# Weight quantization of a transformer layer: three operations a chunk for four, and chunks in sixteen groups of six for four of 24

## The reference

```python
x = _layernorm(x + attn(x, head_dim_mask, w_q, w_k, w_v, w_o))
x = _layernorm(x + ffn(x, w_gate, w_up, w_down))

def _weight_quant(w):        # forward value: wq
    scale = 1.0 / jnp.clip(jnp.mean(jnp.abs(w)), 1e-05)
    wq = jnp.clip(jnp.round(w * scale), -1.0, 1.0) / scale
def _act_quant(x):
    scale = 127.0 / jnp.clip(jnp.max(jnp.abs(x), axis=-1, keepdims=True), 1e-05)
    xq = jnp.clip(jnp.round(x * scale), -128.0, 127.0) / scale
gate = silu(act_quant(x) @ weight_quant(w_gate).T);  up = act_quant(x) @ weight_quant(w_up).T
out  = act_quant(gate * up) @ weight_quant(w_down).T
```

## Time and profile before

| | |
|---|---|
| median of 3 runs | 4197.9 us (4190.73 to 4200.52) |
| profiled execution | 4206.66 us, span of the slowest core 4205.1 us |
| spans of the 8 cores | 4170.1 to 4205.1 us |
| phase AB / C1 and C2 in that span | 1563.4 us / 2641.7 us |
| busy shares in the span | PE 50%, PEld 22%, DVE 56%, ACT 13%, POOL 5% |
| DMA | 440.44 MB, mean 105 GB/s |
| second pass over the weights | DVE 814.8 to 919.4 us and three more stretches like it, the last to 1471.7 us |

### The profile page before, as it was taken

How to read it: one execution, slowest core, us unless ns; L and a number is a source line. 1 busy time by engine, 2 the same in 40 slices (tenths; PEclk the granted TensorE clock), 3 DMA queues, 4 the chain that set the end, 5 groups by cost and what they waited for, 6 DMA issues and landing times. The chain is left out here.

```text
span 4205.1 us, 32766 instructions; the slowest of 8 cores (4170.1 to 4205.1 us)
## 1 busy us (share of the span) xinstructions
PE 2109.6 (50%) x8516; PEld 943.0 (22%) x8516; DVE 2353.7 (56%) x3982; ACT 535.4 (13%) x794; POOL 217.5 (5%) x295
## 2 busy tenths in 40 slices
PE   3625235233241508384747565665747155555555
PEld 2311112111010103232323222222223122222222
DVE  2154661777778755757575766666666522333333
ACT  0211112111020201111111111111111100000000
POOL 1000000111110100000000000000000000000000
PEclk8655555555555559697878778787969577887777
DMA  8315330353443624343333334333423332222222
GB/s 244 116 36 175 115 115 20 95 155 113 127 143 102 182 67 126 91 117 94 100 106 99 105 90 120 83 118 80 130 70 91 96 99 75 85 80 80 80 80 85
DMA packets 290772, 440.44 MB, mean 105 GB/s; under 512 B 12960, under 2 KB 220832, under 8 KB 290592
## 3 DMA queue, kind: packets, MB, share of 16 engines
q1 hardware_dynamic: 250000, 319.32, 25.8%
q0 software_dynamic: 40592, 119.03, 9.7%
HBM read 337.64 MB, written 100.66 MB: 104 GB/s over the span
## 5 line engine op out<-in xcount | busy, mean ns | idle before, releaser
L929 PE MATMUL ps_y<-wdq,hqr 128*128 128x512 bf16 x2048 | 478.6, 397 | 381.4 <-DMA hqr<-hqTs 375.7
L779 PE MATMUL ps_g<-wgu,xqr 128*128 128x512 bf16 x2048 | 495.9, 386 | 132.3 <-issue 92.6
L785 PE MATMUL ps_u<-wgu,xqr 128*128 128x512 bf16 x2048 | 485.1, 380 | 0.0
L799 PE MATMUL ps_t<-identb,hq 128*128 128x128 bf16 x1024 | 129.5, 307 | 582.3 <-DVEq L739 456.1
L53 DVE SCALAR_TENSOR_TENSOR z2t<-ps_y,yscale,x1r 128x512 f32<-128x512 f32 x64 | 48.0, 751 | 561.2 <-PEq L934 482.9
L929 PEld LDWEIGHTS ps_y<-wdq,hqr 128*128 128x128 bf16 x2048 | 205.6, 101 | 654.2 <-issue 438.7
L53 DVE TENSOR_SCALAR gtr<-ps_g,scv 128x512 f32<-128x512 f32 x256 | 192.1, 750 | 249.1 <-PEq L790 248.7
L566 PE MATMUL ps_h<-pbuf,vtok 128*128 128x512 f32 x256 | 195.9, 765 | 244.7 <-ACTq L54 244.7
L53 DVE TENSOR_TENSOR hp<-sgt,ps_u 128x512 f32<-128x512 f32 x256 | 176.0, 687 | 242.5 <-ACTq L54 242.5
L779 PEld LDWEIGHTS ps_g<-wgu,xqr 128*128 128x128 bf16 x2048 | 184.4, 98 | 439.2 <-issue 262.7
L53 ACT ACTIVATE sgt<-gtr 128x512 f32<-128x512 f32 x256 | 161.1, 629 | 873.8 <-DVEq L54 873.8
(11 more groups left out here) (102 smaller groups left out, 2287.0 us busy)
## 6 DMA issues: line engine op xcount, KB each, us to landing
wgu<-wgqs SPq DMA_DIRECT2D x64, 1024.0 KB, 7.8
wgu<-wuqs SPq DMA_DIRECT2D x64, 1024.0 KB, 10.1
wstf<-wgT SPq DMA_DIRECT2D x64, 512.0 KB, 4.9
wstf<-wuT SPq DMA_DIRECT2D x64, 512.0 KB, 4.6
wstf<-wdT SPq DMA_DIRECT2D x64, 512.0 KB, 3.8
hqTs<-hqts POOLq DMA_DIRECT2D x32, 1024.0 KB, 8.7
hqr<-hqTs SPq DMA_DIRECT2D x32, 1024.0 KB, 8.9
xts<-xT POOLq DMA_DIRECT2D x8, 2048.0 KB, 14.2
```

The source lines that it names most:

```text
L779: t.matmul(ps_g[:, sc % 2, :], xqr[:, sb % 2, ic, sc * 128:(sc + 1) * 128], wgu[:, idx % 2, 0, ic, :], start=(ic == 0), stop=(ic == NHC - 1))
L785: t.matmul(ps_u[:, sc % 2, :], xqr[:, sb % 2, ic, sc * 128:(sc + 1) * 128], wgu[:, idx % 2, 1, ic, :], start=(ic == 0), stop=(ic == NHC - 1))
L799: t.transpose(ps_t2[:, k * 128:(k + 1) * 128], hq[:, gsc % 2, oc * 128:(oc + 1) * 128], identb[:])
L929: t.matmul(ps_y2[:, sc % 2, hf, :], hqr[:, pr % 2, oc, (sc % 2) * DH:(sc % 2 + 1) * DH], wdq[:, oc, hf * 512:(hf + 1) * 512], start=(oc == ...
```

## The change

One chunk of the second pass has three DVE operations instead of four. The multiply into `wu_` goes, and the two compares read the loaded weights themselves, against bounds that lie in a new tile `whm`: half of each mean in columns 0 to 3, and minus half of it in columns 4 to 7. `whm` is made once, in `qb` 4.

The chunks also move. Instead of 24 in front of the row sums of each of `qb` 4 to 7, DVE does six behind each of the token chunks 16 to 31. POOL's stores move with them, six behind each of these token chunks. The order of the chunks, the buffers and the semaphores stay.

```diff
--- before.py
+++ after.py
@@ -193,6 +193,7 @@
         ps_tr = PS("ps_tr", [P, 1024], BF16)
         identr = SB("identr", [P, P], F32R)
         ones_r = SB("ones_r", [P, 1], F32R)
+        whm = SB("whm", [P, 8], F32)
         pv32 = ps_vt[:].bitcast(F32)
         blk = es.enter_context(nc.Block())
         @blk.sync
@@ -279,8 +280,8 @@
                     gp.wait_ge(sm["xqsp0" if qb % 2 == 0 else "xqsp1"],
                                16 * NHC * (qb // 2 + 1))
                 _xo(sc + 2)
-                if sc % 4 == 3 and sc >= 15:
-                    wsp_chunks(24)
+                if sc >= 16:
+                    wsp_chunks(6)
             wsp_chunks(len(wsched))
 
         @blk.vector
@@ -330,12 +331,10 @@
                     v.wait_ge(sm["wst0" if ch % 2 == 0 else "wst1"],
                               16 * (len(wsched) // 2 + ch // 2 + 1))
                     wch = wstf[:, ch % 2, 0:n]
-                    v.tensor_scalar(wu_[:, 0:n], wch, wsv[:, 4 + wi:5 + wi],
-                                    None, ALU.mult)
-                    v.tensor_scalar(wc1[:, 0:n], wu_[:, 0:n], 0.5, None,
-                                    ALU.is_gt)
-                    v.tensor_scalar(wc2[:, 0:n], wu_[:, 0:n], -0.5, None,
-                                    ALU.is_lt)
+                    v.tensor_scalar(wc1[:, 0:n], wch, whm[:, wi:wi + 1],
+                                    None, ALU.is_gt)
+                    v.tensor_scalar(wc2[:, 0:n], wch, whm[:, 4 + wi:5 + wi],
+                                    None, ALU.is_lt)
                     if ch >= 2:
                         v.wait_ge(sm["wqsp0" if ch % 2 == 0 else "wqsp1"],
                                   16 * (ch // 2))
@@ -364,8 +363,10 @@
                 if qb == 4:
                     v.wait_ge(sm["wbc"], 1)
                     v.tensor_copy(wsv[:], pv32[:, 4:12]).then_inc(sm["wsc"], 1)
-                if qb >= 4:
-                    w2_chunks(24)
+                    v.tensor_scalar(whm[:, 0:4], wsv[:, 0:4], 0.5, None,
+                                    ALU.mult)
+                    v.tensor_scalar(whm[:, 4:8], wsv[:, 0:4], -0.5, None,
+                                    ALU.mult)
                 v.wait_ge(sm["avrs"], (qb + 1) * 32)
                 v.tensor_copy(rsb[:], ps_r[:])
                 v.reciprocal(rinv[:], rsb[:]).then_inc(sm["rdone"], 1)
@@ -436,6 +437,8 @@
                     v.scalar_tensor_tensor(xqdq[:, sc % 2, :], tiq[:], -128.0,
                                            c1q[:], ALU.add, ALU.add
                                            ).then_inc(sm["xqd"], 1)
+                    if sc >= 16:
+                        w2_chunks(6)
             w2_chunks(len(wsched))
 
         @blk.scalar
```

## The result

| | before | changed |
|---|---|---|
| median | 4195.3 us (8 runs, 4190.7 to 4202.3) | 4384.5 us (8 runs, 4380.8 to 4393.6) |
| ratio | | 1.0452, 95% interval 1.044 to 1.0464 |
| profiled execution, span of the slowest core | 4205.1 us, core 5 | 4425.1 us, core 6 |
| the same, core 5 | 4205.1 us | 4371.1 us |
| core 5: phase AB / the rest | 1563.4 / 2641.7 us | 1746.4 / 2624.7 us |

4377 us had been forecast, and a change of +179 us; the medians lie 189 us apart. In the profiled execution of the changed kernel cores 6 and 7 spent some 35 us more in phases C1 and C2 than the other six cores; in the runs without a profile no core took over 4392.1 us. So core 5 is read here, the core of the rows of before.

A forecast was written before the change was run, and what follows sets the result against it. In the first phase, TensorE waits for DVE's row sums, and DVE's token chunks delay attention. -93.8 saved, +256 exposed runs, +17 tail give +179: 4386, less 8.8, 4377 us; own range 4355 to 4400, with rivals 4338 to 4425.

The forecast's parts named there:

- Saved, 93.8 us: TensorE's waits before the rinv transposes in query blocks 4 to 7 fall to 4.48 us each, saving 93.8 us.
- The exposed runs, 256 us: Twelve six-chunk runs on DVE between token chunks are fully exposed: nine of 21.7 us, three of 20.3, together 256 us.
- L: Time from a load buffer's release to its next chunk's start: 4.9 us for w_gate and w_up, 4.2 for w_down.
- The compare, 0.75 us: In each weight chunk, a DVE compare reading its bound from a whm column takes 0.75 us, like the old multiply.
- Rival B: In the exposed runs, compares slow to 1.23 us, or stores are late: +50 us, 4427 us; chance 0.15.
- Late stores: In exposed runs, chunks' last operations wait for slow stores: 1.2 us on two waits per run, 29 us, range only.
- The tail, 17 us: After token chunk 31, six chunks and their stores follow GpSimd's wait for the xqTs spill, adding 17 us.
- Hidden runs: Runs behind token chunks 19, 23 and 27 cost nothing: about 30 us beside 82.9 us of attention.
- Rival A: Loads in the exposed runs get quicker until DVE alone sets the pace: 18.5 us a run, +145, 4343 us; chance 0.15.
- Rival C: A higher TensorE clock grant in phases two and three pays back the longer slow phase: 4052 to 4190 us; chance 0.03.
- Rival D: Runs between token chunks hide in DVE's own waits, at most 3 us; given no time of its own.
- another time of these phases: Sign of being wrong: phases two and three, expected unchanged at 2642 us, take a different time.

## Why the prediction was right

**Saved, 93.8 us.** All four waits are at 4.48 us, so the term is exact on core 5. That core was on the high side: over the eight cores of the same execution the term is 88.5 to 95.3 us, 90.3 in the mean.

**The exposed runs, 256 us.** 261.8 were measured on core 5, and 260.9 to 268.3 on the eight cores. The form of the term (first two chunks preloaded, the rest at L plus one chunk) is shown from three sides: two chunks cost 6.3 us, six with a fourth operation 24.2 without the gap, six without loads 18.5. L can be read in the trace, from the end of a run's second chunk to the start of its fourth, and from the fourth to the sixth: 4.9 us on core 5 for w_gate and w_up, as taken, and 4.4 for w_down, where I had 4.2. (w_down begins at chunk 64 and not 60, but the count of nine and three runs is right.) L makes 1.5 of the missing 6 us. The other 4 are in the chunks themselves: most take 2.95 us and not 2.89, and a few wait for a store. On the other cores L is from 0.2 us shorter to 0.4 us longer.

**The compare, 0.75 us.** Measured 753 ns in the median. Rival B (1.23 us) is out. Late stores, its other half, cost 1.3 us in all twelve exposed runs of core 5, and 0.3 to 4.3 on the eight cores: 37.1 of DVE's 38.4 us of waiting for stores on core 5 are at three block starts, beside attention, and in the tail. That DVE's compares keep POOL from its stores is not seen either: without loads, with the same compares beside it, no issue of a store took over 0.56 us on any core; with loads the longest took 1.05.

**The tail, 17 us.** Measured +20.5. The sum took POOL to be free at the same time in both kernels, and the hand-over as unchanged. Before, the last spill of `xqTs` lands 2.2 us after its issue, 8.9 us after the end of `xqdq`, and the next phase starts 6.9 us later. Now it lands 5.0 us after its issue, 12.2 us after the end of `xqdq`, with loads of w_down in flight: 3.3 us more. Then 0.6 us pass to the first store, the six stores take 15.8 us (1722.91 to 1738.71), where I had 17 with that step in it, and the hand-over is 7.7 us, 0.8 more. 3.3 + 0.6 + 15.8 + 0.8 is the 20.5. The kernel without loads shows that the loads hold `xqTs`: 2.5 us to its landing there.

**Hidden runs.** Taken as free; from the end of a block's last `xqdq` to the start of `rsb` it is 84.7 us on every core from query block 3 on, with six chunks or, in block 3, none.

The sum for core 5 is -93.8 + 261.8 + 20.5 = +188.5 us, and phase AB got 183.0 us longer; the difference lies ahead of the change, where the row sums of query block 2 came 6.1 us sooner in that execution. From the row sums of query block 3 to the end of phase AB it is 189.1 us more on core 5 and 189 to 199 on the eight cores. The medians say +189. The forecast's +179 is 10 short. Its three errors, taken on the mean of the cores (3.5 us too much saved, 8 too little for the runs, 3 for the tail), all go one way, so none of them hid another, and the mechanism is the one that the runs show.

**Rival A** (DVE alone sets the pace, 4343 us) is what the kernel without loads does, and only that one: 4347. The Trainium skill's fit in "DMA: Bandwidth & Descriptors" ("Anatomy of one DMA"), 2.0 us plus bytes over 436 GB/s, is stated for transfers that GpSimd issues, and these loads go through SyncE; the estimate of 3.2 us that it gives, which would lead to rival A, isn't what they show at eight cores: in the changed kernel they land 4.4 us after issue in the median, 3.2 at the least. For the stores the same fit gives an estimate of 2.6 us, and there the trace agrees once nothing loads beside them (2.6 us), and doesn't when something does (4.7).

**Rival C** (the clock pays it back, 4052 to 4190) is out: the grant on core 5 is 0.92 in the first 155 us of C1 and 0.79 over the two phases, the same as before, after a phase that was 183 us longer at 0.50.

**Rival D** got nothing: the 0.27 us in front of `z1t` are there with two, six and no chunks.

What I had left as it was, phases C1 and C2, is 2620 to 2626 us on cores 0 to 3 in both profiles. On the other four it isn't constant: core 5 has 2641.7 us before and 2624.7 now, core 6 has 2628.4 and 2661.9. On core 5 the number of matmuls, the busy time and the grant are the same; what moves it is not shown. The prediction had named another time of these phases as a sign of being wrong; on these cores it came, in both directions, while the medians' +189 is about what phase AB accounts for by itself.

The change is one gain and one loss: three operations are worth 22 us (ratio 0.9947), and the sixteen runs behind the token chunks, twelve of them exposed, cost 211.

## What to carry to other kernels

Filler work belongs where its engine waits for another, and as much of it as that wait is long: 19 chunks fit beside 83 us of attention, 24 stuck out by 19 to 29 us in each block, and six in a chain that the engine itself sets stuck out whole, 22 us each time. Cutting a block of filler into smaller pieces is no help if the pieces go into that chain. And when filler is paced by a double-buffered load, an operation taken out gives only part of its time (0.26 and 0.39 us of 0.72 here), while the chunks loaded beforehand are the cheap ones (3.1 us against 3.9 for the others of a run).

## What the runs showed of the hardware that I had not expected

- With all eight cores doing the same, a store of 256 KB from POOL lands 2.6 to 2.7 us after issue without loads in flight and 4.5 to 5.0 us with 512 KB loads beside it (medians by core).
- The hand-over from one phase to the next takes 6.2 to 7.7 us by kernel, in one kernel the same on all eight cores, and 7.7 with a store just issued or not.
- The start of attention lies between 144 and 170 us over the eight cores of the ten profiles, though nothing ahead of it differs between the kernels. That is more than the eight runs of the kernel before lie apart (12 us), so a difference of phase lengths is better read from one landmark of the same execution to the next.
- A compare with its bound in a column takes 0.753 us, the operation that compares and subtracts 1.284 us, for 128 x 1024 f32.
